# A fused SSM mixer and expert layer on one core: the bias product as two stacked fp32r products ahead of the y blocks

## The reference, cut to what matters

```python
z_gated = silu(x @ Wz) @ Wzg
y = ssd_scan(X, delta, B, C, A_log) + D_param * X        # 8 heads of 64
x = layernorm(x + (y * z_gated) @ Wout)
dw1, dw2, dw3 = (route_dense(x @ P_w.T @ U.T, 3) for U in (U1, U2, U3))   # weights of the best 3 of 12
h = gelu(sum_e dw1[:, e] * (x @ W1[e].T))                # 128 -> 512
y = sum_e dw2[:, e] * (h @ W2[e].T) + dw3 @ b2           # 512 -> 128
x = layernorm(x + y)
```

## Time and profile before

| | |
|---|---|
| median of three runs | 1539.86 us |
| the profiled execution's own time | 1538.53 us |
| its span, first to last instruction | 1536.8 us |
| PE busy | 1519.4 us (99%) |
| DVE / POOL / ACT busy | 73% / 43% / 39% |
| mean granted TensorE clock | 0.998 of full speed |

### The profile page before, as it was taken

The page is one execution under the profiler, slowest core; times in us unless marked ns, Lnnn a source line. Parts: engine busy times, 40 slices in busy tenths (PEclk is TensorE's granted clock), DMA queues, the critical chain, the costliest instruction groups (busy, mean ns, idle before and its releaser), DMA issues.

```text
span 1536.8 us, 25382 instructions
## 1 busy us (share of the span) xinstructions
PE 1519.4 (99%) x8646; PEld 1252.3 (81%) x8646; DVE 1115.9 (73%) x3113; ACT 597.8 (39%) x1360; POOL 656.2 (43%) x751
## 2 busy tenths in 40 slices
PE   9999999999999999999999999999999999999998
PEld 7778888888888888888788888888888888887886
DVE  7767776877768677686777768777686776867755
ACT  6643524424244351533525244342443515335130
POOL 6671633616246171543616336162461715436040
PEclk9999999999999999999999999999999999999999
DMA  5350312314123040321403213041230403204020
GB/s 179 101 150 28 108 53 59 108 27 125 30 71 97 29 138 15 96 78 40 120 25 111 53 57 111 25 125 33 70 98 29 139 15 94 79 27 135 21 77 7
DMA packets 81456, 114.53 MB, mean 75 GB/s; under 512 B 10144, under 2 KB 37296, under 8 KB 81328
## 3 DMA queue, kind: packets, MB, share of 16 engines
q1 hardware_dynamic: 81328, 112.92, 25.4%
HBM read 107.76 MB, written 5.13 MB: 73 GB/s over the span
## 4 chain that ended last, share of the span: by engine, by line
PE 92%; POOL 3%; DVE 1%; issue 1%; DMA 1%; ACT 1%; SPq 0%; POOLq 0%; DVEq 0%
PE exp_bank L247 23%; PE exp_bank L249 22%; PE exp_bank L248 22%; PE mix_bank L895 4%; PE mix_bank L935 4%; PE mix_bank L247 3%; PE mix_bank L249 3%; PE mix_bank L248 3%; PE mix_bank L917 3%; PE mix_bank L793 1%; PE turn_bank L1262 1%; POOL w_lo L445 1%; PE mix_bank L525 1%; PE mix_bank L739 1%; PE mix_bank L1026 1%
## 5 line engine op out<-in xcount | busy, mean ns | idle before, releaser
L1203 POOL TENSOR_TENSOR sp_lo<-fbuf,sp_hi 128x512 fp32r<-128x512 f32 (+2 forms) x201 | 243.1, 1213 | 201.4 <-ACT sp_hi L1199 110.5
L247 PE MATMUL exp_bank<-w_hi,sp_hi 128*128 128x512 f32 x768 | 304.1, 396 | 0.8 <-POOL sp_lo L1255 0.8
L247 PE MATMUL exp_bank<-sp_hi,w_hi 128*128 128x512 f32 x764 | 303.5, 397 | 0.1
L249 PE MATMUL exp_bank<-w_hi,sp_lo 128*128 128x512 f32 x768 | 299.8, 390 | 0.0
L248 PE MATMUL exp_bank<-w_lo,sp_hi 128*128 128x512 f32 x768 | 298.8, 389 | 0.0
L249 PE MATMUL exp_bank<-sp_hi,w_lo 128*128 128x512 f32 x764 | 297.9, 390 | 0.0
L248 PE MATMUL exp_bank<-sp_lo,w_hi 128*128 128x512 f32 x764 | 297.9, 390 | 0.0
L1302 DVE SCALAR_TENSOR_TENSOR acc<-exp_bank,dw,acc 128x128 f32<-128x128 f32 x384 | 132.1, 344 | 137.8 <-PE exp_bank L249 137.2
L1199 ACT CAST sp_hi<-fbuf 128x512 fp32r<-128x512 f32 (+2 forms) x203 | 120.0, 592 | 286.0 <-DVE fbuf L1169 230.3
L856 POOL TENSOR_TENSOR Wt<-Wt,Gh 128x512 f32<-128x512 f32 x128 | 183.2, 1433 | 11.3 <-DVE Wt L848 11.3
L247 PEld LDWEIGHTS exp_bank<-sp_hi,w_hi 128*128 128x128 f32 x764 | 143.5, 188 | 38.8 <-issue 8.9
(11 more groups left out here) (267 smaller groups left out, 2274.7 us busy)
## 6 DMA issues: line engine op xcount, KB each, us to landing
row_b<-dw_rows SPq DMA_DIRECT2D x189, 256.0 KB, 3.4
seg_b<-dA_rows SPq DMA_DIRECT2D x124, 256.0 KB, 3.6
ctd<-cum_rows SPq DMA_DIRECT2D x128, 96.0 KB, 3.1
x_in<-in_x SPq DMA_DIRECT2D x16, 256.0 KB, 2.7
result<-acc SPq DMA_DIRECT2D x15, 256.0 KB, 2.2
fbuf<-in_W1T SPq DMA_DIRECT2D x12, 256.0 KB, 3.7
acc<-in_W2T SPq DMA_DIRECT2D x5, 256.0 KB, 3.5
x_in<-in_W2T SPq DMA_DIRECT2D x5, 256.0 KB, 3.2
```

The costliest lines, as they stand in the source:

```text
L247: nc.tensor.matmul(ps, s_hi, m_hi, start=start and j == 0, stop=False, skip_group_check=onto)
L249: last = nc.tensor.matmul(ps, s_lo, m_hi, start=False, stop=stop and j == n - 1, skip_group_check=onto)
L1203: sig("xw_lo", on.tensor_tensor(lo[:, cols], wide[e % 2][:, cols], hi[:, cols].bitcast(F32), ALU.subtract))
```

## The change

It has four parts.

1. The bias product. `b2` is split into hi and lo (`split_b2`), `dw3` as well, and the three cross terms are stacked along the contraction: 3 parts x 2 chunks x 12 experts = 72 rows behind the 48 rows of `dw1`. Two chunks go into one product, so there are two fp32r products of 256 columns in place of one f32 product of 512. This takes two transposes in `route_rows`, three more DVE operations in `route_weights`, and a second ACT copy (`bias_rows`). Bodies 2 to 15 issue the product ahead of `mix_y_pair(b, 2)`; body 1 and `mixture_alone` leave it in its place.
2. `mix_out` has q outside and the chunk inside, with a wait for each q.
3. `b2` is staged in `St`; `wout` takes the place of `b2_sb` as fourth staging buffer for batch 0 and is loaded in the midst of batch 0. The decay row of head 7 now lands in the first buffer.
4. The identity is 128 columns wide, not 512.

```diff
-B2ROW = E * NC
+NX2 = NC // 2
+B2ROW, B2LO = E * NC, 3 * P // 4
...
-    [("xT", "xT", 1), ("dwT", "dwT", 1), ("dtB", "dt_raw", 1), ("BC", "BC", 1)]
+    [("xT", "xT", 1), ("dwT", "dw3T", 1), ("dtB", "dt_raw", 1), ("BC", "BC", 1)]
...
-        b2_sb = sb("b2_sb", [P, NC, D])
-
-        ident4, upper = sb("ident4", [P, T]), sb("upper", [P, P])
-        ident = ident4[:, 0:P]
+        b2_tab = sb("b2_tab", [P, NC, D], F32R)
+
+        ident, upper = sb("ident", [P, P]), sb("upper", [P, P])
+        ident_c = ident[:, :].unsqueeze(1).to_broadcast([P, NC, P])
...
-                SP.dma_start(wout[:, :, :], Wout.rearrange("(q p) n -> p q n", p=P)).then_inc(sems["small"], 16)
...
-                PO.memset(b2_sb[:, :, :], 0.0).then_inc(sems["b2_zero"], 1)
+                PO.memset(St[:, :], 0.0).then_inc(sems["b2_zero"], 1)
             if eng is SP:
                 SP.wait_ge(sems["b2_zero"], 1)
-                for c in range(NC):
-                    SP.dma_start(b2_sb[B2ROW + c:B2ROW + E * NC:NC, c, :], b2[:, :]).then_inc(sems["b2_in"], 16)
+                for part in range(3):
+                    for c in range(NX2):
+                        at = B2ROW + (part * NX2 + c) * E
+                        SP.dma_start(St[at:at + E, c * D:(c + 1) * D], b2[:, :]).then_inc(sems["b2_in"], 16)
+
+        def split_b2():
+
+            lo = slice(B2LO, P)
+            both = lambda rows: b2_tab[rows, :, :].rearrange("p (x c) d -> p x (c d)", x=2)
+            DVE.wait_ge(sems["b2_in"], 16 * 3 * NX2)
+            for n in range(2):
+                ins = DVE.tensor_copy(both(slice(0, P))[:, n], St[:, :])
+            ins.then_inc(sems["b2_cut"], 1)
+            DVE.wait_ge(sems["b2_cut"], 1)
+            DVE.tensor_tensor(St[lo, :], St[lo, :], both(lo)[:, 0].bitcast(F32), ALU.subtract).then_inc(sems["b2_cut"], 1)
+            DVE.wait_ge(sems["b2_cut"], 2)
+            for n in range(2):
+                ins = DVE.tensor_copy(both(lo)[:, n], St[lo, :])
+            ins.then_inc(sems["b2_cut"], 1)
...
+                if first(b) and h == 3:
+                    SP.dma_start(wout[:, :, :], Wout.rearrange("(q p) n -> p q n", p=P)).then_inc(sems["wout"], 16)
+                    wait(SP, "scan", b, h + 2)
...
-                wait(PE, "gated", b)
                 ps = mix_bank(b, "out")
-                for c in range(NC):
-                    for q in range(NQ):
-                        last = PE.matmul(ps[:, tok(c)], zg[:, q, tok(c)], wout[:, q, :], start=(q == 0), stop=(q == NQ - 1))
+                for q in range(NQ):
+                    wait(PE, "gated", b, q + 1)
+                    for c in range(NC):
+                        last = PE.matmul(ps[:, tok(c)], zg[:, q, tok(c)], wout[:, q, :], start=(q == 0 and c == 0),
+                                         stop=(q == NQ - 1 and c == NC - 1))
...
-                for r, dst in ((0, cols[:, :, 0:E]), (1, dw2_new[:, :, :]), (2, cols[:, :, E:2 * E])):
+                for r, dst in ((2, dw3), (0, dw1_cols.rearrange("p (e c) -> p c e", c=NC)), (1, dw2_new[:, :, :])):
...
-                sig("dwr", last)
+                wait(DVE, "dw3", b, 1)
+                DVE.tensor_copy(dw3_cols[:, 2], dw3_x)
+                sig("dw3", DVE.tensor_copy(dw3_cols[:, 0], dw3_x))
+                wait(DVE, "dw3", b, 2)
+                sig("dwr", DVE.tensor_tensor(dw3_cols[:, 1].bitcast(F32), dw3_x, dw3_cols[:, 0].bitcast(F32), ALU.subtract))
...
-                sig("ps_dwT", PE.transpose(ps[:, 0:P], dwpad[:, :, :].rearrange("p e c -> p (e c)"), ident[:, :]))
+                for n in range(2):
+                    last = PE.transpose(ps[:, tok(n)], dwpad[:, n, :].bitcast(F32), ident[:, :])
+                sig("ps_dwT", last)
...
-                sig("dwT", AC.copy(rows[:, :], bank_of("dwT", b)[:, 0:P]))
+                sig("dwT", AC.copy(rows[0:E * NC, :], bank_of("dwT", b)[0:E * NC, 0:P]))
                 wait(AC, "ps_b2", b.prev())
+                sig("dw3T", AC.copy(bias_rows[:, :, :], bank_of("dwT", b)[:, 0:2 * P].rearrange("p (x t) -> p x t", x=2)))
...
-                sig("ps_b2", PE.matmul(rb[:, :], rows[:, :], b2_sb[:, :, :].rearrange("p c d -> p (c d)"), start=True, stop=True))
+                for n in range(2):
+                    cols = slice(n * NX2 * D, (n + 1) * NX2 * D)
+                    last = PE.matmul(rb[:, cols], bias_rows[:, n, :],
+                                     b2_tab[:, n * NX2:(n + 1) * NX2, :].rearrange("p c d -> p (c d)"), start=True, stop=True)
+                sig("ps_b2", last)
...
             if not norm_before and eng is DVE:
+                split_b2()
                 DVE.wait_ge(sems["unit"], 1)
...
+            if norm_before and eng is PE:
+                expert_b2(PE, p)
             mix_y_pair(eng, b, 2)
```

More of the change, by code:

```diff
@@ L129, in layer_program @@
         Xde = Wt[:, :, :].rearrange("p a b -> p (a b)")[:, 0:(NC - 1) * DI].rearrange("p (c n) -> p c n", c=NC - 1)
-        rows = sb("rows", [P, P])
+        rows, bias_rows = sb("rows", [P, P]), sb("bias_rows", [P, 2, P], F32R)
         row_b = [sb(f"row_b{n}", [P, T]) for n in range(2)]
@@ L150, in layer_program @@
         dw2_new, dw2 = sb("dw2_new", [P, NC, E]), sb("dw2", [P, NC, E])
-        dwpad = sb("dwpad", [P, WCOLS, NC])
+        dwpad = sb("dwpad", [P, 2, P], F32R)
+        dw1_cols = dwpad[:, 0, 0:E * NC].bitcast(F32)
+        dw3_cols = dwpad[:, :, B2ROW:B2ROW + 3 * NX2 * E].rearrange("p x (q c e) -> p q x c e", q=3, c=NX2)
+        dw3 = fbuf[:, 3, T // 2:T // 2 + NC * E].rearrange("p (c e) -> p c e", c=NC)
+        dw3_x = dw3.rearrange("p (x c) e -> p x c e", c=NX2)
         st6, mv, nrm = sb("st6", [P, NC, 6]), sb("mv", [P, NC, 2]), sb("nrm", [P, 6, NC])
@@ L180, in layer_program @@
             ps_yw=NQ, ps_yq=NQ, gated=NQ, ps_out=1, v=1,
-            ln1_v=7, ln1_s=2, x1=1, ps_x1T=1, x1T=1, ps_lg=1, lg=1, rt_v=8, rt_s=1, dw=1, ps_dwT=1, dwT=1,
+            ln1_v=7, ln1_s=2, x1=1, ps_x1T=1, x1T=1, ps_lg=1, lg=1, rt_v=8, rt_s=1, dw=1, ps_dwT=1, dwT=1, dw3T=1, dw3=2,
             ps_h=E - 1, ps_h_full=NH, gelu=NH,
@@ L466, in second_weights_ready @@
             if eng is PE:
[L467 removed]
+                PE.wait_ge(sems["b2_cut"], 3)
             if eng in (PE, AC, DVE):
@@ L485, in router_product @@
             if eng is PE:
-                PE.wait_ge(sems["small"], 16 * 5)
+                PE.wait_ge(sems["small"], 16 * 4)
                 PE.wait_ge(sems["pad"], 5)
@@ L833, in layer_program @@
         first_seg = [seg_b[0][:, :], seg_b[1][:, :], acc[:, :, :].rearrange("p c d -> p (c d)"),
-                     b2_sb[:, :, :].rearrange("p c d -> p (c d)")]
+                     wout[:, :, :].rearrange("p q d -> p (q d)")]
+        first_seg = first_seg + first_seg[0:3] + first_seg[0:1]
         def mix_decay(eng, b, h):
@@ L847, in mix_decay @@
                     wait(DVE, "ps_yw", b, q - 1)
-                sig("scan", DVE.tensor_tensor_scan(W, first_seg[h % 4] if first(b) else seg_b[h % 2][:, :], unit[:, :], 0.0, ALU.mult, ALU.add))
+                sig("scan", DVE.tensor_tensor_scan(W, first_seg[h] if first(b) else seg_b[h % 2][:, :], unit[:, :], 0.0, ALU.mult, ALU.add))
             ahead = 4 if first(b) else 2
@@ L1088, in spread_weight @@
                 for c in range(NC):
-                    last = PE.transpose(spread_bank[e][:, tok(c)], dwpad[:, e, c:c + 1].to_broadcast([P, P]), ident[:, :])
+                    last = PE.transpose(spread_bank[e][:, tok(c)], dw1_cols[:, e * NC + c:e * NC + c + 1].to_broadcast([P, P]), ident[:, :])
                 last.then_inc(sems["spread"], 1)
@@ L1259, in expert_b2 @@
             if eng is PE:
-                wait(PE, "dwT", b)
+                wait(PE, "dw3T", b)
                 wait(PE, "xw", b)
-                sig("ps_b2", PE.matmul(rb[:, :], rows[:, :], b2_sb[:, :, :].rearrange("p c d -> p (c d)"), start=True, stop=True))
+                for n in range(2):
[3 more added lines that the diff above has]
+                sig("ps_b2", last)
             if eng is DVE:
@@ L1351, in body @@
             elif eng is PE:
-                wait(PE, "dwT", p)
+                wait(PE, "dw3T", p)
                 wait(PE, "Xd", b, 4)
@@ L1367, in body @@
                 wait(AC, "xw", p, 3)
-                AC.copy(unit[:, :], ident4[:, :]).then_inc(sems["unit"], 1)
+                AC.copy(unit[:, :].rearrange("p (c t) -> p c t", c=NC), ident_c).then_inc(sems["unit"], 1)
             if not norm_before and eng is DVE:
+                split_b2()
                 DVE.wait_ge(sems["unit"], 1)
@@ L1435, in body @@
                 second_weights_ready(eng)
-            expert_b2(eng, p)
+            if not norm_before or eng is not PE:
+                expert_b2(eng, p)
             mix_out(eng, b)
@@ L1519, in start_pe @@
             mix_X(PE, nxt, [0])
+            PE.wait_ge(sems["wout"], 16)
             mix_out(PE, b)
```

22 lines of the change are left out of this document (11 added, 11 removed).

## The result

Over 14 runs of each on the same chips the changed kernel takes 1542.89 us (1541.23 to 1543.69), the kernel before 1539.76 us (1536.71 to 1540.48). The ratio is 1.0023, with a 95% interval of 1.0016 to 1.0031: slower by about 0.2%. The prediction said 1542.2 us. The profiled execution took 1543.24 us and its span is 1541.4 us, 4.6 us over the span before; a single pair of profiles differs by more than the medians do (3.1 us).

A forecast was written before the change was run, and what follows sets the result against it. PE, 92% of the chain, was taken as the bound, with DVE's split chain close behind. Terms -1.4 + 1.65 + 0.3 + 1.8 = +2.35 us gave 1540.9 profiled, 1542.2 us as median; range 1538.0 to 1546.5.

The forecast's parts named there:

- What bounds a body: Body's end: PE, but DVE's splits are ready only 0.49 us before the first W2 product's k = 3 wants them.
- The bias product: Two 256-column products at 0.23 us for 0.96; 0.10 us left in each of 14 bodies, -1.4 us.
- the rival at the f32 price: Bias product: 256 columns cost what f32 does, 0.96 in all; +12.6 us, 1552.4; chance 0.05.
- Second transpose: Routing weights on PE: one more step of 0.11 us in each of 15 bodies, unhidden, +1.65 us.
- The bank of `BC`: `BC` waits for ACT's second copy: 0.02 us in 14 bodies, +0.3 us, bounds 0 and +1.1.
- Start-up: Before body 1's bias product: b2 loads and split less identity, +2.4, three quarters arriving: +1.8 us, bounds -0.4 and +3.2.
- Two more loads: +1.6: Start-up on SP: two b2 loads more, at 0.8 us each, delay the loads and weights behind them.
- The slack before 117.35: Body 1's wait for the last `w_lo`: PE has 1.06 us of its own to lose, against a slower outcome.
- the slower case: Start-up delay arrives in full and PE's gap grows: +4.5 us, 1544.3; chance 0.33.
- The slower rival's clock: Body 1's y: if PE's wait grows over one microsecond, more runs at half clock, at most +2; chance 0.33.
- Rule weighed: Start-up: `split_b2` beside POOL, sharing SBUF interfaces, would take some 2.8 us, not 1.3; sum near +3.9.
- the main forecast: Whole kernel: no measurable change, the split chain takes back the bias product's saving; 1539 to 1542.9, chance 0.50.

The follow-up runs named there:

- e1: Kernel before, with the f32 bias product ahead of the last y blocks in bodies 2 to 15 and the output by q: 1547.22 us, ratio 1.0050.
- e3: Changed kernel, with three of DVE's hidden-block splits ahead of the gating of q = 2 and 3 in bodies 2 to 15: 1537.21 us, ratio 0.9984.
- e8: Kernel before, with only DVE's order altered: three hidden-block splits ahead of the gating: 1538.89 us, ratio 0.9999.
- e10: Changed kernel, with only b2's clearing and six loads moved into batch 0, `split_b2` staying in body 1: 1542.53 us, ratio 1.0018.
- e2: Changed kernel, with the two stacked bias products put back between y and the output in all bodies: 1539.73 us, ratio 0.9995.
- e7: Changed kernel, with one transpose and a half-width bias copy, leaving out two chunks' bias weights (for time alone): 1539.78 us, ratio 1.0000.
- e9: Changed kernel, with three DVE splits ahead of the gating and the stacked product behind y: 1533.45 us, ratio 0.9957.
- e4: Changed kernel, with b2 loaded in the first 15 us and split by DVE ahead of batch 0's first scans: 1544.23 us, ratio 1.0028.
- e5: Changed kernel, with b2 cleared, loaded and split in the midst of batch 0: 1541.74 us, ratio 1.0014.

## Why the prediction was right, point by point

- **What bounds a body.** Right, and to some hundredths. Counted from the last expert product the last `lo` was to come 0.23 us later and PE to stop at k = 3, 0.21 us earlier than before and with 0.11 lost again; measured are 0.25, 0.18 and 0.11. e1, e3 and e8 show it from three sides: the wait grows if y comes later, goes if the splits do, and the same edit does nothing while there is slack.
- **The bias product.** 0.23 us for both, my value; the rival at the f32 price (0.96) is out. Of the 0.73 us saved on PE the wait for the gating (0.26), the longer output product behind it (0.09), the wait at k = 3 (0.20) and the longer step behind that (0.11) leave 0.07, where the prediction had 0.10. Over all 36 W2 products behind it 0.04 is left (16.43 to 16.39). The term is -0.6 instead of -1.4.
- **Second transpose.** 0.11 us as priced.
- **The bank of `BC`.** An under-sized term: 0.06 us in each body, where I took 0.02 with 0.08 as the bound. I had let the copies overlap "a little"; they overlap by 0.10 us (0.26 long, 0.16 apart), but PE's restart came 0.15 us behind the second one's end and not 0.05. +0.8 instead of +0.3.
- **Bodies in sum.** -0.04 + 0.11 + 0.06 is +0.13, as measured by the medians, 1.8 us over 14, where the prediction had +0.4 for them (14 times -0.10 + 0.11 + 0.02). Six of these distances in the changed profile and three before are 0.2 to 0.4 us longer than the rest, by single stops of PE; that is the step from 1.8 to the 2.40 us between the two profiles. What causes these stops stays open.
- **Start-up.** The size came near by chance (+1.8 forecast, 1.67 us at the output of body 1 in the two profiles), the parts did not. Of the 3.1 us between the medians of the runs, the bodies' 1.8 and the 0.5 behind the last output leave some 0.8 for the start-up, an estimate; so the sum came out near because the start-up was forecast too high and the bodies too low. The step that failed is "Two more loads: +1.6": I priced each load at the 0.8 us of the earlier trace rows, but six took 2.35 us, and e10, without them there, is no faster by a difference that can be told. The split cost PE about 1.05 (+1.2 forecast), the identity gave back 0.66 us at PE's first matmul (2.23 to 1.57), and 0.23 was left of it at batch 0's output (48.05 to 47.82). At the expert product at 76 us the changed kernel is 0.54 us ahead of the kernel before (76.07 and 76.61), so the row of head 7 and the later load of `wout` show no cost there; no run took them apart.
- **The slack before 117.35.** I held against the slower case that PE has 1.06 us to lose there. It lost none of them: the last `w_lo` came 2.25 us later, PE only 1.60, and the wait grew to 1.73 us. The slack is on PE's side, and what was late was the chain that PE waits for.
- **The slower rival's clock.** The rest of the delay, 1.17 of the 1.67 us, is a longer stretch at half the granted clock. Its condition, a wait longer by a microsecond, was wrong. The wait is 3.2 to 3.3 us in all twelve profiles, and the low stretch there is nothing in two of them, about 3.4 us in six and about 6.8 in four. Busy time by engine in that stretch, first of the changed kernel:

```profile
95.00:101.00 6.00, 5.65 (x42) 4.86 (x43) 1.58 (x4) 1.28 (x4) 3.89 (x4) 0.50 0.34 115
```

and of e10:

```profile
96.00:99.50 3.50, 3.50 (x43) 2.94 (x39) 1.99 (x4) 0.74 (x4) 3.13 (x3) 1.00 0.37 132
```

Behind POOL's group stands the granted clock: 0.50 in the changed kernel, as 0.51 in the earlier trace rows, is the level of 1.2 GHz, 1.00 in e10 that of 2.4 GHz. From the first y block to the next expert product PE needs 6.9 us in e1 and e10, which had no low stretch, 7.85 before and 9.02 in the changed profile. So a single profile carries 0 to 2 us here that vary with the clock. The long stretch stands in four of the six profiles that have `split_b2` in body 1 (the changed kernel, e2, e3, e7; not e9 and e10) and in none of the other six. That is too few to say whether the change makes it more frequent.
- **Rule weighed.** `split_b2` met no POOL work in the changed kernel (1.41 us), as the main forecast had it. Where it does meet it, in e4, it takes 5.0 us, more than the 2.8 that I worked out from the earlier trace rows. The casts suffer as the subtraction does: three of the four take 1.02, 1.13 and 1.27 us and each ends 0.15 us behind the end of a POOL instruction (24.36, 25.41, 28.13); the fourth, behind POOL's last, takes 0.29. The Trainium skill, "SBUF — State Buffer", section "SBUF: two separate sides", says that the pair of ports that VectorE and GpSimd share is locked for a whole instruction, not divided, and that an fp32 copy within SBUF is of the kind that takes it; the trace of e4 agrees.

## What to carry to other kernels

Before an instruction is made cheaper or moved, ask what it covers: here a product of 0.96 us hid the gating, and 0.49 us of slack at a second chain was the most that could be won without touching that chain. A product that nobody waits for belongs behind the work that starts the other engines' chain, not ahead of it; then put those engines' ready work ahead of what they still have to wait for. The change as made cost 0.23%; the same parts in another order, DVE's splits included, gained 0.46%.

## What the runs showed of the hardware

- Two fp32r products of 256 columns take a step of 0.12 us, and 0.21 us to the f32 matmul that follows; the f32 product of 512 columns took 0.96.
- A restart behind DVE's `lo` costs PE the wait and 0.11 us more in the step behind it: 0.34 instead of 0.23 us in the bodies of the changed kernel. Its weight load starts with the matmul there (both at 406.73), where in the stream it starts a step ahead.
- Small fp32 to fp32r casts on DVE, 128 x 256, take 0.29 us each with POOL idle and 1.02 and 1.13 us beside POOL's multiplications.
- The length of a queue's row of DMA issues is no price of an issue: loads of b2 took 0.8 us each in the kernel before, 0.39 in the changed one, and 0.58 in e5 (3.47 us for six). What makes the difference isn't shown.
